# First stage of a two-layer decoder kernel: matmuls on zeros ahead of the loads, a divided weight load, another order of angles, and weight differences moved into the state-space rounds

## What is computed

```python
# part 1, _L0_attn_ref: D_INNER = 512, N = 64, H = 8 heads, 16 rotated pairs
zxbcdt = x @ W_in                                   # 256 -> 512 (z) + 512 (xs) + 64 (B) + 64 (C) + 8 (dt)
dt = softplus(dt_columns + dt_bias)
decay = exp(-exp(A_log) * dt)
angle = dt[..., None] * inv_freq;  cos, sin = cos(angle), sin(angle)
# scan over tokens: h = decay * rotate(h, cos, sin) + dt * B (x) xs;  y = h . C
y = (y + D_skip * xs) * silu(z)
y = y * rsqrt(mean(y * y) + 1e-5) * norm_weight
x = layernorm(x + y @ W_out)
# part 2, _L0_xattn_ref: 16 heads of 64
q, k, v = x @ Wq, context @ Wk, context @ Wv
x = layernorm(x + softmax(q k^T / 8) v @ Wo + bo)
```

## Time and profile before

| what | value |
|---|---|
| median of three runs | 1054.21 us (1052.16, 1054.21, 1057.50) |
| the profiled execution | 1052.41 us |
| its span, first to last instruction | 1050.6 us |
| mean granted clock of TensorE | 0.978 of full |
| busy share: TensorE, its weight loads, VectorE, ScalarE, GpSimd | 93%, 72%, 55%, 39%, 14% |
| first stage | 0 to 33.2 us |
| state-space stage | 33.2 to 124.5 us |
| first layer's cross-attention begins | 125.5 us |

### The profile page before, as it was taken

How to read it: one execution, slowest core, us unless ns; L and a number is a source line. 1 busy time by engine, 2 the same in 40 slices (tenths; PEclk the granted TensorE clock), 3 DMA queues, 4 the chain that set the end, 5 groups by cost and what they waited for, 6 DMA issues and landing times. The chain is left out here.

```text
span 1050.6 us, 17783 instructions
## 1 busy us (share of the span) xinstructions
PE 978.9 (93%) x6554; PEld 756.4 (72%) x6554; DVE 579.3 (55%) x1306; ACT 411.7 (39%) x1077; POOL 150.5 (14%) x151
## 2 busy tenths in 40 slices
PE   6899789999999999977999999898889999999985
PEld 4587677877777778657899999375567677777663
DVE  1878545555555565554855656247735444545544
ACT  2465524333343333324454544256633223323221
POOL 0243510110110100002344331210010000000000
PEclk9999899999999999987999999899999999999998
DMA  4500100000000000006521100440000000000000
GB/s 152 194 2 1 45 21 1 17 16 1 15 0 0 0 0 0 0 1 226 164 80 40 40 1 20 109 78 2 1 20 15 15 15 16 4 12 24 6 5 18
DMA packets 26542, 36.18 MB, mean 34 GB/s; under 512 B 3632, under 2 KB 22144, under 8 KB 26480
## 3 DMA queue, kind: packets, MB, share of 16 engines
q1 hardware_dynamic: 26480, 35.35, 11.4%
HBM read 30.75 MB, written 2.75 MB: 32 GB/s over the span
## 5 line engine op out<-in xcount | busy, mean ns | idle before, releaser
L1080 ACT ACTIVATE x_prob<-bank,x_negmax 112x375 f32<-112x375 f32 x128 | 72.2, 569 | 155.3 <-DVE x_negmax L996 155.3
L1805 DVE TENSOR_TENSOR moe_h_low<-moe_sq,moe_h_high 128x512 fp32r<-128x512 f32 (+1 forms) x64 | 55.4, 886 | 49.3 <-ACT moe_h_high L1907 35.5
L1882 POOL TENSOR_TENSOR moe_sq<-moe_r 128x512 f32<-128x512 f32 (+1 forms) x64 | 64.4, 1010 | 111.3 <-ACT moe_r L1916 89.6
L996 DVE TENSOR_REDUCE x_negmax<-bank 112x1 f32<-112x375 f32 x128 | 64.1, 542 | 9.1 <-PE bank L888 7.1
L101 PE MATMUL bank<-moe_w_high,moe_h_high 128*128 128x256 f32 x224 | 63.4, 283 | 0.2 <-DVE moe_shifted L1764 0.2
L101 PE MATMUL bank<-moe_w_low,moe_h_high 128*128 128x256 f32 x224 | 63.4, 283 | 0.0
L101 PE MATMUL bank<-moe_w_high,moe_h_low 128*128 128x256 f32 x224 | 63.3, 283 | 0.0
L1916 ACT ACTIVATE moe_r<-bank 128x512 f32<-128x512 f32 (+1 forms) x64 | 34.8, 545 | 72.6 <-PE bank L101 68.1
L909 PEld LDWEIGHTS bank<-x_prob_t,x_v 125*64 125x64 f32 x768 | 38.0, 139 | 34.9 <-issue 30.9
L1001 DVE COPY x_prob_t<-bank 125x336 f32<-125x336 f32 x128 | 59.0, 499 | 5.7 <-PE bank L897 3.7
L888 PE MATMUL bank<-x_kt,x_qt 64*112 64x375 f32 x256 | 58.2, 532 | 0.7 <-DVE x_kt L988 0.7
(11 more groups left out here) (368 smaller groups left out, 2265.7 us busy)
## 6 DMA issues: line engine op xcount, KB each, us to landing
moe_w<-in_L_ffn_W SPq DMA_DIRECT2D x15, 512.0 KB, 4.8
ctx_t<-in_ctx_t SPq DMA_DIRECT2D x8, 376.0 KB, 4.8
x_ctx_t<-in_ctx_t SPq DMA_DIRECT2D x8, 376.0 KB, 3.2
wk<-in_L_xattn_Wk SPq DMA_DIRECT2D x2, 1024.0 KB, 6.4
wv<-in_L_xattn_Wv SPq DMA_DIRECT2D x2, 1024.0 KB, 9.1
wq<-in_L_xattn_Wq SPq DMA_DIRECT2D x2, 1024.0 KB, 11.2
wo<-in_L_xattn_Wo SPq DMA_DIRECT2D x2, 1024.0 KB, 13.1
w_in<-in_L_attn_W_in SPq DMA_DIRECT2D x1, 1160.0 KB, 7.1
```

Source lines behind the costliest of these rows:

```text
L996: dve.tensor_reduce(negmax[:, g:g + 1], S_BANK(u, e)[0:T, 0:S], AX_X, ALU.max, negate=True).then_inc(max_ready, 1)
L1080: act.activation(PROB(u, e)[:, :], S_BANK(u, e)[0:T, 0:S], ACT.Exp, bias=negmax[:, g:g + 1], accum_out=total[:, g:g + 1]).then_inc(p_ready, 1)
L1805: dve.tensor_tensor(h_low[half][:, m, 0:size], sq[m % 2][:, 0:size], h_high[half][:, m, 0:size].bitcast(F32), ALU.subtract).then_inc(low_d ...
L1882: pool.tensor_tensor(sq[m % 2][:, 0:size], r[m % 2][:, 0:size], r[m % 2][:, 0:size], ALU.mult).then_inc(sq_done, 1)
```

## The change

**Loads.** `w_in` comes in two DMAs: columns 0 to 511 (the gate) with `w_loaded`, the rest with a semaphore of its own. **Zeros.** VectorE first writes zeros into `whole`, a buffer of 112x1024 that the angles use later, and TensorE does three 512-column matmuls on it into bank 7 before it waits for any load. **Order on TensorE:** zeros, z(0), dt, z(1), z(2), time, z(3) to z(7). **VectorE:** `w_out` is scaled after the angles. **ScalarE:** sine and cosine stand ahead of the last silu. **State space:** the keys' casts move from round 7 to 6 and the values' from 8 to 7; VectorE makes the keys' differences in round 7, one between variance and gate and one between decay_scores and normalize, and the values' in round 8 in the same places. **Cross-attention:** the four differences and the waits for `w_split` go.

```diff
-        ZB = 4
+        w_rest_loaded, zeros_ready = core.sem("p1_w_rest_loaded"), core.sem("p1_zeros_ready")
+        ZB, WARM = 4, 3
...
-                sp.dma_start(core.w_in[:, :, :], d["L0_attn_W_in"].rearrange("(c p) n -> p c n", p=128)).then_inc(w_loaded, 16)
+                w_in = d["L0_attn_W_in"].rearrange("(c p) n -> p c n", p=128)
+                sp.dma_start(core.w_in[:, :, 0:DI], w_in[:, :, 0:DI]).then_inc(w_loaded, 16)
+                sp.dma_start(core.w_in[:, :, DI:W_IN], w_in[:, :, DI:W_IN]).then_inc(w_rest_loaded, 16)
...
+                def warm():
+
+                    zeros = whole[:, :, :].rearrange("t g p -> t (g p)")
+                    pe.wait_ge(zeros_ready, 1)
+                    for k in range(WARM):
+                        pe.matmul(bank[7][0:T, :], zeros[:, 0:T], zeros[:, 512:1024], start=True, stop=True)
+
+                warm()
                 pe.wait_ge(x_loaded, 16)
                 pe.wait_ge(w_loaded, 16)
+                z(0)
+                pe.wait_ge(w_rest_loaded, 16)
                 for i in range(B):
                     last = accumulate(pe, bank[0][0:T, i * H0:(i + 1) * H0], [
                         (core.xt[:, c, i * T:(i + 1) * T], core.w_in[:, c, W_IN - H0:W_IN]) for c in range(KD)])
                 last.then_inc(dt_ready, 1)
-                for i in range(ZB):
-                    z(i)
+                z(1)
+                z(2)
                 pe.wait_ge(core.loaded, 32)
                 pe.wait_ge(steps_ready, 1)
...
-                for i in range(ZB, B):
+                for i in range(3, B):
                     z(i)
...
+                dve.memset(whole[:, :, :], 0.0).then_inc(zeros_ready, 1)
...
-                dve.wait_ge(w_out_loaded, 32)
-                dve.tensor_tensor(core.w_out[:, :, :], core.w_out[:, :, :], core.w_norm[:, :].unsqueeze(2).broadcast_to([128, 4, D]),
-                                  ALU.mult).then_inc(w_scaled, 1)
-                dve.wait_ge(w_scaled, 1)
...
                 dve.tensor_tensor(cos_in[:, :, :], cos_in[:, :, :], whole[:, :, :], ALU.subtract).then_inc(angles_ready, 1)
+                dve.wait_ge(w_out_loaded, 32)
+                dve.tensor_tensor(core.w_out[:, :, :], core.w_out[:, :, :], core.w_norm[:, :].unsqueeze(2).broadcast_to([128, 4, D]),
+                                  ALU.mult).then_inc(w_scaled, 1)
...
                 for i in range(B):
+                    if i == B - 1:
+                        act.wait_ge(angles_ready, 1)
+                        act.activation(sine[:, :, :], sin_in[:, :, :], ACT.Sin, scale=TURN)
+                        act.activation(cosine[:, :, :], cos_in[:, :, :], ACT.Sin, scale=TURN)
                     act.wait_ge(z_ready, i + 1)
                     act.activation(zs[:, i, :], bank[1 + i % ZB][0:T, :], ACT.Silu).then_inc(z_used, 1)
-                act.wait_ge(angles_ready, 1)
-                act.activation(sine[:, :, :], sin_in[:, :, :], ACT.Sin, scale=TURN)
-                act.activation(cosine[:, :, :], cos_in[:, :, :], ACT.Sin, scale=TURN)
...
+                def difference(n, w, rest):
+
+                    dve.wait_ge(w_rounded, 2 * "kv".index(n) + rest + 1)
+                    to, high = (core.w_rest_low, core.w_rest) if rest else (core.w_low, core.w_high)
+                    dve.tensor_tensor(to[n][:, :], w[:, rest, :], high[n][:, :].bitcast(F32), ALU.subtract)
+
+                parts_of = {B - 1: ("k", core.wk), B: ("v", core.wv)}
                 for r in ROUNDS:
...
+                    if r in parts_of:
+                        difference(*parts_of[r], 0)
                     if there(r - 1):
                         gate(r - 1)
                     if there(r):
                         decay_scores(r)
+                    if r in parts_of:
+                        difference(*parts_of[r], 1)
...
+                    if r == B - 2:
+                        round_weights("k", core.wk)
                     if r == B - 1:
-                        round_weights("k", core.wk)
-                    if r == B:
                         round_weights("v", core.wv)
...
-                            if not heads:
-                                pe.wait_ge(w_split, 1)
...
-                        if a == 0 and not heads:
-                            pe.wait_ge(w_split, 2)
...
-                for name, w in (("k", core.wk), ("v", core.wv)):
-                    dve.tensor_tensor(w_low[name][:, :], w[:, 0, :], w_high[name][:, :].bitcast(F32), ALU.subtract)
-                    dve.tensor_tensor(w_rest_low[name][:, :], w[:, 1, :], w_rest[name][:, :].bitcast(F32),
-                                      ALU.subtract).then_inc(w_split, 1)
                 rounds(dve, round_)
```

More of the change, by code:

```diff
@@ L402, in state_space @@
             sem("var_ready"), sem("rstd_ready"), sem("normed_ready"), sem("x_copied"), sem("nt_ready"), sem("nt_copied"))
-        rounded, act_chain, log_taken = sem("rounded"), sem("act"), sem("log_taken")
+        rounded, act_chain, log_taken, w_rounded = sem("rounded"), sem("act"), sem("log_taken"), sem("w_rounded")
         Y, TURNED, XS, BC, LOG, OUT = bank[0], bank[1:3], bank[3], bank[4], bank[5:7], bank[7]
@@ L671, in round_weights @@
                     act.wait_ge(core.xw_loaded, 80)
-                    act.copy(core.w_high[n][:, :], w[:, 0, :])
-                    act.copy(core.w_rest[n][:, :], w[:, 1, :])
+                    act.copy(core.w_high[n][:, :], w[:, 0, :]).then_inc(w_rounded, 1)
+                    act.copy(core.w_rest[n][:, :], w[:, 1, :]).then_inc(w_rounded, 1)
                 for r in ROUNDS:
@@ L804, in cross_attention @@
         dve_chain, act_chain = sem("dve"), sem("act")
-        split_chain, split_done, w_split = sem("split_chain"), sem("split_done"), sem("w_split")
+        split_chain, split_done = sem("split_chain"), sem("split_done")
         bias_added = sem("bias_added")
```

## The result

The changed kernel takes 1044.56 us at the median against 1054.21 of the kernel before. The ratio is 0.9898 with a 95% interval of 0.9861 to 0.9935: 10.7 us less, with 6.9 to 14.7 in the interval. One of the changed kernel's five executions took 1231.41 us at a granted clock of 0.741 and is left out of the ratio. The forecast was 1048.6 within 1044.0 to 1052.5. The sign was right. The gain was about twice the 5.6 us of the sum. The profiled execution took 1043.35 us, its span is 1041.5 against 1050.6.

The account below looks back on a forecast made before the run. TensorE, busy 93% of the span, was taken as the bound, except in three places. Terms 4.0 + 1.0 - 1.6 + 2.25 = 5.6 us took the median from 1054.2 to 1048.6, range 1044 to 1052.5.

Parts of the forecast that it names:

- the sum: Whole kernel: 4.0 from the first stage, 1.0 from sines, less 1.6 in the tail, plus 2.25 in cross-attention, 5.6 us gained.
- The fall of the clock: First stage: TensorE's clock drops to half near the narrow group's end, costing 1.8 us and leaving 4.0 of 5.8.
- The tail: Last state-space rounds: the four moved differences on VectorE cost 0 to 3.5 us, taken as 1.6.
- Zeros and loads: First stage: zeros from 1.8 raise the clock and split loads start z(0) at 6.9; gain 5.8 us if it stays up.
- three other rises: Clock rises seen 3.3 us (first stage), 5.1 (cross-attention queries) and 5.6 (mixture) after wide matmuls; gave 5.1 to 7.4.
- The likeliest case: First stage: the clock falls once; chance 0.48, with its own range of 1046 to 1051 us.
- The rival in which it stays up: First stage: the clock does not fall after the narrow group; gain 7.4 us, time 1046.8, chance 0.30.
- The sines: End of the first stage: sine and cosine ahead of the last silu let ScalarE end sooner, gaining 1.0 us.
- the second difference: State-space tail: VectorE's difference ahead of `normed` costs 1.2 + 0.8 for a block - 0.6 to spare = 1.4 us.
- Cross-attention: Start of cross-attention: TensorE's two waits around the first key job, 0.62 and 1.63 us, go; gain 2.25 us.
- The rival on the slower side: State-space tail: differences blocked beside GpSimd take 5.58 us each; 6.3 us slower, 1060.5, chance 0.03.
- The zeros-without-effect rival: First stage: zeros don't raise the clock, nothing gained there, 1.6 us remain, 1052.6; chance 0.16 including late loads.

## Why the prediction was right and wrong, step by step

**What failed, in short.** The mechanisms were mostly right, and three terms of the sum were not. The fall of the clock was charged as certain, at 1.8; it came in one of four profiles and cost 1.6 there, 0.4 on the mean of four. The tail was charged at 1.6; at the same clock it cost under 0.1. And whatever the change moves in time behind the second key job was put at nothing without a reason; the four profiles of each kernel differ by 2.6 us there, in ranges that overlap, so how much of it belongs to the change stays open.

**Zeros and loads: right.** The memset took 0.91 us, within 0.4 to 1.3, and the zeros started at 1.99 against 1.8. z(0) started at 6.96 (6.9), the rest of `w_in` was there at 8.53 (8.4), and the narrow group took 3.5 us (3.5). That zeros raise the clock was a reading of three other rises. It held: the clock rose at 5.5 to 8.3 us with them (5.1 to 7.4 was forecast), and at about 10 without. The Trainium skill ("TensorE: Matmul & The Clock Gate", section "Terms") names a monitor that watches how busy TensorE is; that matmuls on zeros brought the rise forward agrees with it.

**The fall of the clock: the step that failed.** The likeliest case had it fall once, near the narrow group's end, for 1.8 us. The size was right: 27.56 against 25.93 is 1.6. Its chance was not. It fell in one of the four profiles of the changed kernel and two of ten with its order. The first profile happened to have it, at the place forecast, so that profile alone would have confirmed the step by luck. The evidence in hand was 16 narrow records in the mixture that ended at half clock, with a pause behind them, and the prediction said that the two could not be told apart. These runs show each of them: the clock fell behind the narrow group with no pause in four of twelve profiles, and around a pause in the single load (1.88 us) and in half of the six profiles with 2.82 us. Neither brings it about each time, and what decides is open. The rival in which it stays up, put at 0.30, was the common outcome; its gain of 7.4 still held the tail's 1.6. In it TensorE ends the stage at 25.94 - 1.60 = 24.34, where the forecast had 24.6.

**The sines: slightly low.** 1.2 us (2.82 to 1.60) for 1.0. The two sines overlap on ScalarE's timeline (24.77 to 25.82 and 25.72 to 26.76), and the last silu ended at 27.25, 1.3 behind where the pause says TensorE did (27.56 - 1.60 = 25.96).

**The tail: mis-sized.** It was priced at 1.6 (0 to 3.5) and cost 0.03 at the same clock (92.36 against 92.33). The term that failed is the second difference, 1.2 + 0.8 - 0.6 = 1.4. It did take 1.21, at 107.01. But `normed` behind it took 0.59 and not the 1.23 of the earlier trace rows: 0.41 is normal for it, and GpSimd's `ctx_low` ran beside that 1.23, from 111.86 to 113.78, so it already held a wait. The block was counted once in the row and once more as an addition, and in fact it was replaced. From s2, `normed` ended at 80.69 before and at 81.17 now: 0.48 us later, inside the 0.6 that the prediction had found to spare. GpSimd's work had moved, because the first difference held it up: `ctx_high` took 1.50 us at 103.70 beside `wk_low`, which itself took 1.97. The end of `wk_low` at 104.85 stands 0.1 ahead of `y`, so nothing was late. `turn_state` came at 108.86, 5.70 earlier than in the earlier trace rows, and s2 was 5.68 earlier: the tail cost nothing. By the Trainium skill's rule on who waits ("SBUF — State Buffer", section "Who interferes with whom") the difference waits only for what is left of one GpSimd instruction. That agrees in kind and about in size: `decay` had 0.9 us to go at 102.88, and the difference took 1.97 against 1.21 us. In the mean of four profiles q - s2 is 0.45 longer, because in two of them the clock fell at 112.7 and not at 117.5 or later; that came from the clock and not from the differences.

**Cross-attention: low by a little.** At equal query time (6.21 and 6.24) k1 - q shrank by 2.65 where 2.25 was forecast. The two waits were 2.25. A further 0.26 went since the first key job starts 0.23 before the queries' modelled end, and the rest as that job takes 0.94 and not 1.08. The query copy sits at 126.17 and hides, as the prediction had it. The remainder to the mean gain of 3.0 is queries that ran partly at full clock. Before, k1 - q was 9.57 or 9.58 whether the queries took 6.24 or 6.57 us, because VectorE's differences ended last; now it goes with the queries' clock, 6.14 to 7.11.

**The sum.** With the clock up and the tail free, the prediction's own terms give 5.8 + 1.0 + 2.25 = 9.05, and the landmarks gave 9.7. The sum failed by the case it chose and by the tail. The low end of the range, 1044, was this very pair, the clock up and the tail hidden. It held nothing for the clock behind the landmarks. 9.7 from 1054.2 would be 1044.5, inside the range; the last 1.0 of the 10.7 lies behind k1, where one stretch in cross-attention goes with the moved differences (0.7 to 1.9 us) and the rest isn't resolved. That is where the range ended too high.

**The chances.** Faster by over 0.5% had the largest chance, and it was so. The rival on the slower side did not come: the longest difference took 1.97 us and not 5.58. The zeros-without-effect rival (0.16) was wrong in its premise and in its price, as the run without them shows.

## What to carry to other kernels

Where TensorE starts with a load, let it multiply anything while it waits, and split the load so that its first real work begins as that ends; after a pause of 1.88 us between the two the clock was lost again. Filling the waits of the rounds ahead of a stage kept the clock up for its start in both kernels that did it, and delayed nothing there (92.33 us), though the whole time isn't shown to be shorter. Before pricing an added operation by the waits around it, look whether the long operation in the row is long because it waits already, since an addition may only take that wait's place.

## What the runs showed that was not expected

- The clock's falls differ between executions of one kernel. Of the four profiles of the changed kernel one has a fall at 12.3, two have one at 112.7, and one has neither. But for the one of 1231.41, single executions of it lie between 1038.87 and 1046.19, so one pair of profiles would have mis-sized each part.
- In two of the three profiles of the changed kernel in which the clock stayed up at 12.3 it fell at 112.7. That made q - s2 1.0 to 1.2 us longer, and k1 - q 0.8 shorter, because the clock was back during the queries. That one fall brings on or spares the other is not shown: the kernel without zeros had one at 13.6 and one at 116.0.
- Narrow matmuls (8 columns) didn't raise the clock in 6.2 us, but for 3.5 us they held it in 8 of 10 profiles with the changed kernel's order, and in none of the two with a single load or without zeros.
- The granted clock is shown as 1.00 in the zeros, where 4 records take 3.3 us: ahead of the first event that the trace has of it, the column says nothing.
- A GpSimd cast of one input was slowed as well (1.50 us at 103.70, where 0.50 is usual) when VectorE's two-input difference ran beside it.
